# The state scan's u loads and running sums, and a routing phase whose VectorE program becomes a loop

## The reference

```python
decay = jnp.exp(dt[..., None] * A)
inp = (dt * x)[..., None] * Bm[:, :, None, :]
s = dec * s + ip                      # over the 1024 steps
y = jnp.einsum('bdn,bn->bd', s, c)    # sum over the 16 states
y = y + D_skip * x
```

```python
probs = jax.nn.softmax(mla_out @ router_w + router_b, axis=-1)
topw, topi = jax.lax.top_k(probs, TOPK)
topw = topw / (topw.sum(-1, keepdims=True) + 1e-08)
```

## Time and profile before

| | us |
| --- | --- |
| median of 3 runs | 4495.71 (4488.63 to 4503.1) |
| the profiled execution | 4489.22 |
| its span | 4487.6 |
| TensorE busy | 3613.8 (81%) |
| VectorE busy | 3349.0 (75%) |
| ScalarE busy | 2330.5 (52%) |
| GpSimd busy | 1420.4 (32%) |
| VectorE: 256 scans of 2280 ns | 579.1, idle before them 79.9 |
| GpSimd: 128 scatters of 984 ns | 126.0, idle before them 110.5 |

### The profile page before, as it was taken

One profiled execution on the slowest core, in us unless ns is written; L12 is line 12 of the kernel. 1 busy time (PEld: TensorE's weight loads), 2 busy tenths in 40 slices (PEclk: granted clock), 3 DMA queues, 4 the chain that ended last, 5 costly groups with the idle time before them and its releaser, 6 DMA issues. The chain is left out here.

```text
span 4487.6 us, 70677 instructions
## 1 busy us (share of the span) xinstructions
PE 3613.8 (81%) x19727; PEld 2112.8 (47%) x19728; DVE 3349.0 (75%) x4215; ACT 2330.5 (52%) x4148; POOL 1420.4 (32%) x905
## 2 busy tenths in 40 slices
PE   8968888888447967878689999999999996549960
PEld 3445555554334557767633333333333333449960
DVE  8959888888764446655588888888888874658868
ACT  6755555554773432220037777777777773123323
POOL 4458888888232333220100000000000002645530
PEclk9989999999778988989869999999999996569985
DMA  6754444443657842228412232323232303422249
GB/s 216 251 187 163 156 156 155 155 155 118 220 195 164 198 118 83 65 75 227 140 34 69 49 69 49 69 49 69 49 69 49 68 9 93 126 60 90 91 130 303
DMA packets 534113, 537.43 MB, mean 120 GB/s; under 512 B 84720, under 2 KB 439792, under 8 KB 533664
## 3 DMA queue, kind: packets, MB, share of 16 engines
q1 hardware_dynamic: 507328, 475.20, 36.6%
q0 software_dynamic: 13952, 37.74, 2.5%
q10 hardware_dynamic: 12544, 20.98, 1.8%
HBM read 317.41 MB, written 215.19 MB: 119 GB/s over the span
## 5 line engine op out<-in xcount | busy, mean ns | idle before, releaser
L2085 DVE TENSOR_REDUCE at_top<-at_psM 128x1 f32<-128x1024 f32 x1024 | 1205.9, 1219 | 209.0 <-PE at_psM L1934 208.0
L2044 ACT ACTIVATE at_probs<-at_psS 128x512 f32<-128x512 f32 x2048 | 1068.7, 604 | 336.6 <-PE at_psS L1960 326.0
L1960 PE MATMUL at_psS<-at_q,at_k 64*128 64x512 f32 x2048 | 805.3, 470 | 17.9 <-ACT at_probs L2044 8.2
L568 POOL TENSOR_TENSOR sc_prod<-sc_state,sc_c_row 128x1024 f32<-128x1024 f32 x256 | 707.1, 2779 | 156.5 <-DVE sc_state L717 145.5
L1934 PE MATMUL at_psM<-at_k,at_q 62*128 62x512 f32 x2048 | 680.8, 446 | 50.6 <-DMA at_vraw<-scratch_vf 21.8
L717 DVE TENSOR_TENSOR_SCAN sc_state<-sc_dec,sc_psI 128x1024 f32<-128x1024 f32 x256 | 579.1, 2280 | 79.9 <-PE sc_psI L638 48.5
L1934 PEld LDWEIGHTS at_psM<-at_k,at_q 62*128 62x128 f32 x2048 | 322.0, 192 | 600.6 <-DVE at_top L2085 533.6
L1973 PE MATMUL at_psV<-at_probs,at_v 128*32 128x512 f32 x4096 | 552.9, 612 | 34.2 <-ACT at_sums L2049 32.1
L649 PE MATMUL sc_psY<-sc_prod,sc_ident 128*128 128x512 f32 x1024 | 478.9, 608 | 41.2 <-DVE sc_y L703 35.8
L599 ACT ACTIVATE sc_dec<-sc_dt,sc_a_exp 128x1024 f32<-128x1024 f32 x256 | 293.6, 1148 | 328.3 <-DVE sc_state L717 325.2
L1960 PEld LDWEIGHTS at_psS<-at_q,at_k 64*128 64x128 f32 x2048 | 340.3, 185 | 222.3 <-ACT at_probs L2044 214.6
(11 more groups left out here) (395 smaller groups left out, 5127.9 us busy)
## 6 DMA issues: line engine op xcount, KB each, us to landing
sc_c_row<-scratch_bc SPq DMA_DIRECT2D x128, 512.0 KB
scratch_xs<-at_zeros SPq DMA_DIRECT2D x140, 264.0 KB, 4.7
sc_b_row<-scratch_bc SPq DMA_DIRECT2D x64, 512.0 KB, 5.2
ec_y<-scratch_ys SPq DMA_DIRECT2D x32, 512.0 KB, 6.6
ex_x<-scratch_xs SPq DMA_DIRECT2D x39, 264.0 KB, 3.0
si_x<-in_x SPq DMA_DIRECT2D x16, 512.0 KB, 4.4
scratch_xn<-si_xn SPq DMA_DIRECT2D x16, 512.0 KB, 5.0
scratch_x_t<-si_xT SPq DMA_DIRECT2D x16, 512.0 KB, 5.6
```

The costliest lines, as they stand in the source:

```text
L568: pool.tensor_tensor(prod[:, (n * H + h) % 8, :], state[slot][:], c_row[n % ROWS][:], ALU.mult).then_inc(prod_ready, 1)
L1960: pe.matmul(psS[v % 3][:], rows_of(k4[j], h, 0, GROUP)[:, c * P:(c + 1) * P], rows_of(q4[j], h, 0, GROUP)[:, half * TILE:(half + 1) * TILE ...
L2044: act.activation(probs[:, slot(j, v), :], psS[v % 3][:], ACT.Exp).then_inc(act_done, 1)
L2085: dve.tensor_reduce(top[j % 2][:, h, c:c + 1], psM[t % 2][:], AX.X, ALU.max, negate=True).then_inc(maxed, 1)
```

## The change

In the scan, LAG is 3. u of the next sequence is loaded by a function of its own at SP's state 2, behind the stores of y, and has a semaphore of its own, for which TensorE's transposes and VectorE's mix wait; dt and x stay at state 4 on `loaded`.

```diff
-    LAG = 2
+    LAG = 3
...
+                def load_u(b, k):
+                    for h in two:
+                        sp.dma_start(u[k][h][:], unit("u_t", b, h)).then_inc(u_loaded[k], 16)
+
                 def load(b, k):
                     for h in two:
-                        sp.dma_start(u[k][h][:], unit("u_t", b, h)).then_inc(loaded[k], 16)
                         sp.dma_start(dt[k][h][:], unit("dt_t", b, h)).then_inc(loaded[k], 16)
                         sp.dma_start(x[k][h][:], unit("x_t", b, h)).then_inc(loaded[k], 16)
...
                         if place < 3 and n == 4:
                             load(b + 1, 1 - k)
+                        if place < 3 and n == 2:
+                            load_u(b + 1, 1 - k)
...
+                load_u(0, 0)
                 load(0, 0)
...
-                            pe.wait_ge(loaded[1 - k], (b + 1 - (1 - k)) * 48 + 96)
+                            pe.wait_ge(u_loaded[1 - k], (b + 1 - (1 - k)) * 16 + 32)
                             pe.wait_ge(state_ready, b * PER + (TURN - 1 + h))
                             turn(b + 1, 1 - k, h, psI[h])
...
-                    dve.wait_ge(loaded[k], (b - k) * 48 + 96)
+                    dve.wait_ge(u_loaded[k], (b - k) * 16 + 32)
                     dve.wait_ge(row_loaded[d % 2], b * (NX // 2 * 16) + (d // 2 + 1) * 16)
```

```diff
+        LINKS = 2 * CB + 19
...
-        top = m.sb("top", [P, NP, E])
+        top, best = m.sb("top", [P, NP, 2]), m.sb("best", R)
...
+                    m.settle(dve)
                     for c in range(CB):
-                        step.mark(dve.max(top[:, b * CB + c, :], lg[:, c, :]))
+                        step.mark(dve.max(best[:, c, :], lg[:, c, :]))
                     step.wait(dve)
+                    m.settle(dve)
                     for c in range(CB):
-                        step.mark(dve.max_index(index[:, c, :], top[:, b * CB + c, :], lg[:, c, :]))
+                        step.mark(dve.max_index(index[:, c, :], best[:, c, :], lg[:, c, :]))
                     step.wait(dve)
+                    step.mark(dve.tensor_copy(top[:, cs, :], best[:, :, 0:2]))
...
-                for b in range(B):
-                    tile(b * NB)
-                    tile(b * NB + 1)
-                    if b:
-                        fold(b - 1)
-                        choose(b - 1)
-                        spots(b - 1)
-                fold(B - 1)
-                choose(B - 1)
-                spots(B - 1)
+                def sequence(b, k):
+                    fold(b, k)
+                    choose(b, k)
+                    spots(b)
+
+                def ahead(b, k):
+                    for t in range(NB):
+                        tile(b, t)
+                    sequence(b - 1, k)
+
+                for t in range(NB):
+                    tile(0, t)
+                with dve.Fori(0, (B - 2) // 2) as turn:
+                    for k in two:
+                        ahead(turn * 2 + (k + 1), k)
+                ahead(B - 1, 0)
+                sequence(B - 1, 1)
```

More of the change, by code:

```diff
@@ L472, in ssm_scan @@
         a_made, a_exp_made = m.sem("a_made"), m.sem("a_exp_made")
-        loaded, c_loaded = [m.sem(f"loaded{k}") for k in two], [m.sem(f"c_loaded{k}") for k in range(ROWS)]
+        u_loaded, loaded = ([m.sem(f"{n}loaded{k}") for k in two] for n in ("u_", ""))
+        c_loaded = [m.sem(f"c_loaded{k}") for k in range(ROWS)]
         b_turned, b_ready, u_turned, uT_ready = m.sem("b_turned"), m.sem("b_ready"), m.sem("u_turned"), m.sem("uT_ready")
@@ L593, in batch @@
                             if own == 0:
-                                act.wait_ge(loaded[k], (b - k) * 48 + 96)
+                                act.wait_ge(loaded[k], (b - k) * 32 + 64)
                             if own in (TURN + 2, TURN + 3) and place < 3:
@@ L675, in _ @@
                 last.then_inc(b_turned, 1)
-                pe.wait_ge(loaded[0], 96)
+                pe.wait_ge(u_loaded[0], 32)
                 turn(0, 0, 0, psI[1])
@@ L698, in output @@
                 def output(b, k, h):
-                    dve.wait_ge(loaded[k], (b - k) * 48 + 96)
+                    dve.wait_ge(loaded[k], (b - k) * 32 + 64)
                     dve.wait_ge(y_added, (b + 1) * PER - (1 - h))
@@ L2171, in flat, with one @@
             return ap.rearrange("p a b -> p (a b)")
+        def one(ap):
+            return ap.rearrange("p (a f) -> p a f", a=1)
         def per_chunk(ap):
@@ L2320, in _ @@
             def _(dve):
-                step = Chain(own, 0)
+                step = Chain(own, LINKS)
                 def then(ins):
@@ L2332, in _, with tile @@
                 dve.tensor_tensor(bias[:], psA[:, 2, E:2 * E], rb[:], ALU.add).then_inc(bias_made, 1)
-                def tile(i):
-                    dve.wait_ge(ao_loaded[i % 2], 32 * (i // 2 + 1))
-                    if i >= 2:
+                def tile(b, t):
+                    i = b * NB + t
+                    later = not isinstance(b, int) or b > 0
+                    dve.wait_ge(ao_loaded[t], 32 * b + 32)
+                    if later:
                         dve.wait_ge(aon_ready, i - 1)
-                    dve.reciprocal(rs[i % 2][:], ao[i % 2][:, 1, :]).then_inc(rs_ready, 1)
+                    dve.reciprocal(rs[t][:], ao[t][:, 1, :]).then_inc(rs_ready, 1)
@@ L2339, in tile, with fold @@
                     dve.wait_ge(rs_ready, i + 1)
-                    if i >= 2:
+                    if later:
                         dve.wait_ge(turned, i - 1)
-                    dve.tensor_tensor(aon[i % 2][:], ao[i % 2][:, 0, :], rs[i % 2][:], ALU.mult).then_inc(aon_ready, 1)
-                def fold(e):
+                    dve.tensor_tensor(aon[t][:], ao[t][:, 0, :], rs[t][:], ALU.mult).then_inc(aon_ready, 1)
+                def fold(e, k):
+                    head1_of, own_w1 = (K.w1[part][:] for part in two)
+                    head2_of, own_w2 = (K.w2[part][:].rearrange("p e f d -> p e (f d)") for part in two)
@@ L2345, in fold @@
                     dve.wait_ge(head1, e + 1)
-                    dve.tensor_tensor(K.w1[1][:, e, :], psW[e % 2][:], K.w1[0][:, e, :].bitcast(F32), ALU.subtract).then_inc(rest1, 1)
+                    dve.tensor_tensor(own_w1[:, bass.ds(e, 1), :], one(psW[k][:]), head1_of[:, bass.ds(e, 1), :].bitcast(F32),
+                                      ALU.subtract).then_inc(rest1, 1)
                     dve.wait_ge(head2, e + 1)
-                    dve.tensor_tensor(flat(K.w2[1][:, e, :, :]), flat(raw2[e % 2][:]),
-                                      flat(K.w2[0][:, e, :, :]).bitcast(F32), ALU.subtract).then_inc(rest2, 1)
@@ L2351, in choose @@
-                def choose(b):
-                    cs = slice(b * CB, (b + 1) * CB)
+                    dve.tensor_tensor(own_w2[:, bass.ds(e, 1), :], one(flat(raw2[k][:])), head2_of[:, bass.ds(e, 1), :].bitcast(F32),
+                                      ALU.subtract).then_inc(rest2, 1)
+                def choose(b, k):
+                    step.begin(b)
+                    cs = bass.ds(b * CB, CB)
                     dve.wait_ge(turned, (b + 1) * NB)
                     dve.wait_ge(bias_made, 1)
-                    dve.tensor_tensor(lg[:], logits[b % 2], per_expert(bias[:]), ALU.add).then_inc(lg_made, 1)
+                    dve.tensor_tensor(lg[:], logits[k], per_expert(bias[:]), ALU.add).then_inc(lg_made, 1)
@@ L2393, in spots @@
                     dve.wait_ge(spots_ready, b + 1)
-                for b in range(B):
-                    tile(b * NB)
-                    tile(b * NB + 1)
-                    if b:
-                        fold(b - 1)
-                        choose(b - 1)
-                        spots(b - 1)
-                fold(B - 1)
-                choose(B - 1)
-                spots(B - 1)
+                    step.end()
+                def sequence(b, k):
[13 more added lines that the diff above has]
+                sequence(B - 1, 1)
+                step.base, step.n = B * LINKS, 0
                 dve.wait_ge(folded, E)
```

## The result

The changed kernel takes 4461.96 us (median of 5, 4458.16 to 4467.81) beside 4499.31 for the kernel before, run with it: ratio 0.9921, 95% interval 0.9905 to 0.9937, so 37 us less. Forecast: 4455, 40 us less, range 4424 to 4480. The forecast is 7 us low: 3.1 us of that is the sum, 3.6 the kernel before, whose median was 4495.7 when the forecast was made and 4499.3 with the two later executions. The two profiled executions differ by less: 4464.5 against 4489.2 us, 24.7 us.

The account below looks back on a forecast made before the run. In the scan VectorE sets the pace, so its idle time counts; in routing VectorE and GpSimd alternate. Terms -26.3 -16.1 -2.0 +4 make -40.4 us, 4455 us on the median; range for 8 in 10: 4424 to 4480.

Parts of the forecast that it names:

- Boundary, 26.3: Scan, start of each sequence: LAG 3 cuts VectorE's waits for scan inputs over seven boundaries, 26.3 us less, from 17 to 29.2.
- wait one: Scan boundary: VectorE's 3.23 us idle ahead of scan 4 goes whole; of the next, 1.22 ahead of scan 5, 0.4 stays.
- So I expect the full clock: Scan boundary: TensorE's 5.2 us pause is cut in two by an input, so the granted clock no longer falls to 0.50.
- Turn, 16.1: Scan, mid-sequence transposes of the next u: sooner load and own semaphore cut VectorE's waits, 16.1 us less, from 7 to 17.5.
- idle 1.3, late next is the add: Turn of u: TensorE's add ahead of the transposes becomes the late one, leaving VectorE 1.3 us idle in each of seven turns.
- Start, 2.0, and tail, 0: Scan start: u halves go first, saving TensorE's 2.0 us wait; scan end: three adds instead of two cost 0.
- Loop, +4: Routing as a loop: 3 us in spots and choose(0), 1 for two jumps (0 to 8.3); range -3 (less program to load) to +17.
- the period of 25.7 us: Routing, per sequence: 20.3 us of scatters, 2.4 of late signals, 2.2 for spots and a restart; loop touches only the 2.2.
- rival D: Routing: register-count waits slow VectorE's 20 chained steps a sequence; at 11 us a sequence 4505 us, slower; chance 0.05.
- A: Routing: stalls go with the straight code, so GpSimd's scatters bound it, 31 us gained, 4420 us; chance 0.11.
- B: Scan boundary: the wait only moves, scan 4 still waits about as long and u alone gains, 4480 us; chance 0.08.
- C: Turn of u: u isn't early because SP's y stores wait, so 16.1 is 7 or less, 4464 to 4471 us; chance 0.13.

Follow-up runs that it names:

- e4_loop: Kernel before with only the routing phase turned into a loop, scan as before: 4459.6 us beside 4462.7, ratio 0.9996.
- e1_lag: Kernel before with LAG 3 instead of 2 and nothing else: 4433.5 us beside 4462.7, ratio 0.9938.
- e11_u_sem: Both scan edits with straight routing, but u sent at state 4 ahead of dt and x, still on its own semaphore: 4423.2 us beside 4459.7, ratio 0.9915.
- e5_after: The changed kernel itself, run again on another set's chip beside the kernel before: 4423.7 us beside 4461.1, ratio 0.9916.

## Why the prediction was right, point by point

**Sum: -40.4 forecast, -37.3 measured.** It is nearer than its terms, and that is luck: the scan edits gave 37.4 (35.5 in the stretch and 1.9 at the start) and not 44.4, the loop 0 and not +4, and the two errors have opposite signs. The chances of "faster" add up to 0.91 and not 0.89.

**Boundary, 26.3.** Right in mechanism and place: wait one went whole, and of the second nothing stays where 0.4 was left. In the first pair of traces it is worth 19.4 us: 18.7 less of input waits, of which 1.5 is the start and 3.1 the two turns of the loop, and 5.3 of decay waits. What it lacks is the wait ahead of scan 9, 1.2 to 1.8 us in five sequences, 7.8 in all. "So I expect the full clock" failed: in those five sequences the granted clock fell to its lower level once, at this place. In the four later traces with the same scan code the wait stands in two sequences each, 3.4 us in all, so how much comes back there differs from execution to execution. The 3.1 at the loop's turns were not forecast, and no edit is shown to have won them: those waits are 8.2 us in the trace of before, 6.7 in e4_loop with the same scan code, 5.0 in that of after and 6.3 to 7.2 in the four later traces with its scan code.

**Turn, 16.1.** The step "idle 1.3, late next is the add" held to 0.1 us (1.21), and the waits fell by 17.1. The step that failed is the one behind it, that a wait gone is time won. I asked what is late next on TensorE and not what runs beside the mix when it comes 1.8 us sooner. GpSimd's product ended at 418.5 and the mix came at 419.05, 0.6 us clear of it, and the row at 959.37 above had the price. The stretched mixes took 6.8 us back. The Trainium skill, SBUF — State Buffer, section SBUF: two separate sides, has the rule: a VectorE operation with two SBUF inputs and a GpSimd operation that reads SBUF exclude each other for a whole instruction, and the one that starts first has its way. The traces agree: 2.36 us behind a product, 1.23 with the product held, and 1.09 us, within 0.01, from the product's end to the mix's in all fourteen traces.

**The two were added as if independent.** They aren't: 8.7 us of the turn's wait went with LAG alone. Both edits shorten the same wait. This is the larger error, 8.8 us between 44.3 and 35.5, and it is why the u edit adds 3.8 us behind the other one.

**Start, 2.0, and tail, 0.** First scan at 274.3 us on average in the three traces with the old load, 272.4 in the eleven others: 1.9. From the last scan to the last y it is 8.1 us in every trace.

**Loop, +4.** Too much by medians twice: -3 and +0.2. That something would cover it was right. What covers it is not the late signals, as the step "the period of 25.7 us" had it, but GpSimd's 16 scatters of 1.27 us. In the pair of first traces scatters took 5.9 us longer and began 2.3 us later in their phase, rival D in small; yet the medians there differ by 37.3 us, as in the later set without late signals (37.4). Both have intervals of 7 us to either side, so that a cost of a few us where signals come late is neither shown nor refuted. What makes them late stays open too: no later set met that. The -3 at the range's lower end, for less program to load, is shown by no run.

**Rivals.** A (the stalls go with the straight code, 31 us) did not come true: beside the kernel before they stayed, and in the later sets they are gone from the kernel before too (4460 to 4463 us and not 4499), which has the straight code. B is refuted by e1_lag. C did not come true either: u went out at 388.31 and no transpose waited for a transfer; yet e11_u_sem shows that the sooner transfer is worth nothing. D is refuted where signals come in time (e4_loop, e5_after). By the Trainium skill, Runtime: NRT & Kernel Launch, section Instruction fetch mechanics, a taken branch out of the two blocks held stalls. The page gives no size; the prediction priced such a stall at both jumps at 8.3 us by a row of TensorE, and in the traces VectorE idles 0.67 and 0.70 us at its two jumps back.

**The single traces' 24.7 us** are the scan's 33.9 and the start's 2.1, less 2.7 in phases that were not touched, 2.3 ahead of the scatters, 5.9 in them and 0.5 behind. The execution of before was 10 us under its median, that of after 2.5 over.

## What to carry to other kernels

When a wait is taken away, look up what the engines beside it do at the moment at which the freed instruction will now start, and compare durations as well as waits afterwards: here 6.8 of 17.1 us came back as longer instructions, and one wait on GpSimd, which had time, got them back. Two edits that shorten waits in the same loop are summed only after asking whether the first moves what the second waits for. A bound that rests on signals arriving late may be one of that chip or that hour; before a term is built on it, it has to be seen a second time elsewhere.

## What the runs showed of the hardware

A VectorE multiply of two SBUF operands stood still until a running GpSimd multiply had ended (2.36 and 3.13 us for 1.21), while VectorE's scans, with one operand from the accumulators' memory, took 2.26 to 2.29 us in the trace of before and in that of after, beside a product or not. The order of arrival decides who pays: a mix that comes second ends 1.09 us behind the product's end (49 to 67 mixes a trace), and GpSimd's product takes 3.25 us instead of 2.36 when the mix comes first.

The same program ran 4461.96 us in the first set of runs and 4423.68 in a later one, and the kernel before 4499.3 and 4461.1. Of the 38 us 36 are GpSimd's waits in one phase (118.1 against 82.0 us), where in the first set VectorE's and TensorE's signals came up to 4.9 us late while GpSimd issued scatters (0.15 us at most at the same two places in the later sets). Whether that goes with a chip isn't shown: the record numbers the chips of the later sets (8, 6 and 0) and not that of the first.
